# Half of the late wide cross's keys made earlier, in the narrow cross, and kept in DRAM until they are used

## The reference, cut to what matters

```python
# layer 0, second block: narrow cross attention, 16 heads of 8
q = layernorm(x) @ Wq0.T + bq0;  k = ctx @ Wk0.T + bk0;  v = ctx @ Wv0.T + bv0
x = x + softmax(q k / sqrt(8) + mask) v @ Wo0.T + bo0
...                       # feed-forward of layer 0, two narrow self attentions
# layer 1: wide cross attention, 16 heads of 64, inner width 1024
q = layernorm(x) @ Wq + bq;  k = ctx @ Wk + bk;  v = ctx @ Wv + bv
x = x + softmax(q k / 8) v @ Wo + bo
x = x + tanh(layernorm(x) @ W + bias)      # last block, in the same stage
```

## Time and profile before

| what | value |
|---|---|
| runs | 2460.63, 2465.46, 2465.57 us, median 2465.46 |
| the profiled execution: its time | 2466.49 us |
| its span, first to last instruction | 2464.7 us |
| mean granted TensorE clock | 0.949 of full speed |
| wide cross | about 1708 to 2465 us of the span |
| narrow cross | about 548 to 911 us of the span |

### The profile page before, as it was taken

One profiled execution on the slowest core, in us unless ns is written; L12 is line 12 of the kernel. 1 busy time (PEld: TensorE's weight loads), 2 busy tenths in 40 slices (PEclk: granted clock), 3 DMA queues, 4 the chain that ended last, 5 costly groups with the idle time before them and its releaser, 6 DMA issues. The chain is left out here.

```text
span 2464.7 us, 90437 instructions
## 1 busy us (share of the span) xinstructions
PE 2193.9 (89%) x33039; PEld 1802.1 (73%) x33039; DVE 1921.8 (78%) x5481; ACT 1509.8 (61%) x3973; POOL 1225.4 (50%) x1215
## 2 busy tenths in 40 slices
PE   8999999988777753439999799998999999999998
PEld 7888888875555541228888678886888888888886
DVE  3888888868999986988888667775777778777785
ACT  0666666657777766538888678885344444444443
POOL 0333333327777763019999699995223223232232
PEclk8999999998999996659999899999999999999999
DMA  4000000001111100010000000000000000000000
GB/s 122 3 0 0 0 0 0 0 4 34 30 31 30 29 17 1 1 34 2 0 0 0 1 2 0 0 0 4 9 12 12 13 11 13 11 11 13 11 12 15
DMA packets 66160, 29.87 MB, mean 12 GB/s; under 512 B 19139, under 2 KB 65542, under 8 KB 66054
## 3 DMA queue, kind: packets, MB, share of 16 engines
q1 hardware_dynamic: 62642, 27.26, 4.1%
q10 hardware_dynamic: 3412, 1.19, 0.2%
HBM read 20.04 MB, written 8.39 MB: 12 GB/s over the span
## 5 line engine op out<-in xcount | busy, mean ns | idle before, releaser
L706 POOL TENSOR_TENSOR sa_sc<-sa_sc,sa_rs 128x1024 f32<-128x1024 f32 x64 | 121.9, 1904 | 317.3 <-DVE sa_rs L682 317.3
L1861 POOL TENSOR_TENSOR lo_qk_r<-lo_qk_ms,w_neg_half 128x20 f32<-128x20 f32 x64 | 226.7, 3543 | 22.0 <-DVE lo_qk_ms L1784 21.9
L1861 POOL TENSOR_TENSOR gl_qk_r<-gl_qk_ms,w_neg_half 128x20 f32<-128x20 f32 x64 | 226.9, 3545 | 1.4 <-DVE gl_qk_ms L1784 1.4
L486 POOL TENSOR_TENSOR xan_ve<-xan_mv,w_eps_ln 128x1 f32<-128x1 f32 x64 | 12.1, 189 | 400.2 <-DVE xan_mv L480 400.2
L889 ACT ACTIVATE xan_xT<-xa_misc 128x128 f32<-128x128 f32 x64 | 17.7, 277 | 297.9 <-PE xa_misc L789 267.3
L1012 POOL TENSOR_TENSOR xa_sc<-xa_sc,xa_rs 128x1024 f32<-128x1024 f32 x64 | 121.7, 1901 | 112.2 <-DVE xa_rs L972 112.2
L818 PEld LDWEIGHTS xa_qs<-xan_xT,late_x_wq 128*128 128x128 f32 x1024 | 120.0, 193 | 53.3 <-issue 53.3
L558 PE MATMUL sa_qs<-san_xT,w_a_wq 128*128 128x128 f32 x1024 | 132.2, 284 | 2.6 <-DVE sa_sc L668 2.2
L818 PE MATMUL xa_qs<-xan_xT,late_x_wq 128*128 128x128 f32 x1024 | 132.1, 282 | 0.6 <-DVE xa_sc L963 0.6
L829 PE MATMUL xa_pp<-xa_cT,late_x_wk 128*128 128x128 f32 x1024 | 131.1, 281 | 0.0
L926 ACT ACTIVATE xa_oT<-xa_oo 128x512 f32<-128x512 f32 x128 | 69.4, 594 | 97.6 <-PE xa_oo L865 97.6
(11 more groups left out here) (329 smaller groups left out, 6878.1 us busy)
## 6 DMA issues: line engine op xcount, KB each, us to landing
w_x<-in_x_dram SPq DMA_DIRECT2D x8, 512.0 KB, 7.6
ca_cx<-in_ctx_dram SPq DMA_DIRECT2D x64, 64.0 KB, 1.8
ctxT_kept<-ca_xcT SPq DMA_DIRECT2D x64, 64.0 KB, 1.6
xa_cT<-ctxT_kept SPq DMA_DIRECT2D x64, 64.0 KB, 1.8
out_dram<-xa_out SPq DMA_DIRECT2D x64, 64.0 KB, 1.6
ca_mask<-in_mask_BxSxS_ff_dram SPq DMA_DIRECT2D x64, 32.0 KB, 1.7
w_a_wq<-in_L_attn_Wq_dram SPq DMA_DIRECT2D x1, 512.0 KB
w_a_wo<-in_L_attn_Wout_dram SPq DMA_DIRECT2D x1, 512.0 KB
```

The lines of the kernel that those rows point to most:

```text
L706: pool.tensor_tensor(v, v, bcast(rs[:, s, :], 2, S), ALU.mult).then_inc(prob_done, 1)
L1861: pool.tensor_tensor(qk_r[:, s, :], qk_ms[:, s, :], k["neg_half"][:, 0:NQK], ALU.pow).then_inc(sg["qk_r"], 1)
```

## The change

PE's `keys` in the wide cross makes only the lower four of the eight 128-column blocks; the upper four (columns 512 to 1023) are made in the narrow cross by a new piece `ahead`, copied from PSUM by ACT (`ahead_keys`), stored by SP (`keep_keys`) to a new DRAM buffer of 256 KB per tile, and loaded back by SP in the wide cross (`load_keys`). There DVE adds their bias from SBUF instead of PSUM.

```diff
 wide cross, SP
                 def load(t, s):
-                    after(sp, k_psum, t, 2, per=2)
-                    after(sp, v_psum, t, 2, per=2)
+                    after(sp, k_psum, t, 2)
...
+                def load_keys(t, s):
+                    after(sp, k_done, t, 2, per=2)
+                    sp.dma_start(ak[:, s, :], k["aheadK"][at, :]).then_inc(ak_in[s], 16)
...
-                skewed(sp, NT, [(0, load), (10, store)])
+                skewed(sp, NT, [(0, load), (0, load_keys), (10, store)])
 wide cross, PE
-                    for b in range(2):
-                        after(pe, p_done, t, 2, per=2)
-                        for c in range(4):
-                            ch = 4 * b + c
-                            final = pe.matmul(pp[b][:, c * P:(c + 1) * P], k["x_wk"][:, ch * P:(ch + 1) * P],
-                                             cT[:, s, :], start=True, stop=True)
-                        final.then_inc(k_psum, 1)
+                    after(pe, p_done, t, 2, per=2)
+                    for c in range(4):
+                        final = pe.matmul(pp[0][:, c * P:(c + 1) * P], k["x_wk"][:, c * P:(c + 1) * P],
+                                         cT[:, s, :], start=True, stop=True)
+                    final.then_inc(k_psum, 1)
 wide cross, DVE
                     after(dve, s_psum, t, 2)
-                    for b in range(2):
-                        dve.wait_ge(k_psum, t * 2 + b + 1)
-                        dve.tensor_tensor(kT[:, s, 4 * b:4 * b + 4, :], pp[b][:, :].rearrange("p (c i) -> p c i", c=4),
-                                          bcast(k["x_bk"][:, 4 * b:4 * b + 4], 2, P), ALU.add).then_inc(k_done, 1)
+                    landed(dve, ak_in, t, s)
+                    dve.tensor_tensor(kT[:, s, 4:8, :], ak[:, s, :].rearrange("p (c i) -> p c i", c=4),
+                                      bcast(k["x_bk"][:, 4:8], 2, P), ALU.add).then_inc(k_done, 1)
+                    after(dve, k_psum, t)
+                    dve.tensor_tensor(kT[:, s, 0:4, :], pp[0][:, :].rearrange("p (c i) -> p c i", c=4),
+                                      bcast(k["x_bk"][:, 0:4], 2, P), ALU.add).then_inc(k_done, 1)
 narrow cross, SP
+                def keep_keys(t, s):
+                    after(sp, ak_done, t)
+                    sp.dma_start(k["aheadK"][at, :], ak[:, s, :]).then_inc(ak_out[s], 16)
+                sp.dma_start(wk[:, :], k["dram"]["L1_xattn_Wk"][:, 512:1024]).then_inc(wk_in, 16)
-                skewed(sp, NT, [(2, keep), (0, load)])
+                skewed(sp, NT, [(2, keep), (0, load), (3, keep_keys)])
...
 narrow cross, PE
+                def ahead(t, four):
+                    s = four % 2
+                    after(pe, xT_done, t)
+                    after(pe, ak_done, t, 1)
+                    after(pe, p_done, t, 4, per=2)
+                    for n in range(4):
+                        last = pe.matmul(pp[0][:, n * P:(n + 1) * P], wk[:, n * P:(n + 1) * P], xcT[:, s, P:2 * P], start=True, stop=True)
+                    last.then_inc(ak_psum, 1)
...
                 def turn_probs(t, four):
                     after(pe, exp_done, t)
+                    pe.wait_ge(ak_done, min(t + 4, NT) if isinstance(t, int) else t + 4)
...
-                skewed(pe, NT, [(3, scores), (2, project), (1, turn), (6, attend), (5, turn_probs), (7, output)], 4)
+                pe.wait_ge(wk_in, 16)
+                skewed(pe, NT, [(3, scores), (2, project), (2, ahead), (1, turn), (6, attend), (5, turn_probs), (7, output)], 4)
 narrow cross, ACT
                     after(act, qkv_psum, t, 2)
+                    after(act, ak_psum, t, 2)
                     landed(act, kept, t, s, 2)
...
+                def ahead_keys(t, four):
+                    s = four % 2
+                    after(act, ak_psum, t)
+                    landed(act, ak_out, t, s, 2)
+                    act.activation(ak[:, s, :], pp[0][:, :], ACT.Copy).then_inc(ak_done, 1)
...
-                skewed(act, NT, [(2, queries_keys), (1, turned), (2, values), (4, exponent), (5, probsT), (0, apply)], 4)
+                skewed(act, NT, [(2, queries_keys), (2, ahead_keys), (1, turned), (2, values), (4, exponent), (5, probsT), (0, apply)], 4)
 build
+    k["aheadK"] = nc.dram_tensor("ahead_keys", (tiles * P, 512), F32, kind="Internal").ap()
```

More of the change, by code:

```diff
@@ L726, in wide_cross_attention @@
         cT = sb("cT", [P, 2, P])
+        ak = sb("ahead_keys", [P, 2, 512])
         qT = sb("qT", [P, 2, 8, P])
@@ L742, in wide_cross_attention @@
         ctx_in = [sem(f"ctx_in{s}") for s in range(2)]
+        ak_in = [sem(f"ahead_in{s}") for s in range(2)]
         q_psum, q_done, k_psum, k_done, v_psum, v_done = sem("q_psum"), sem("q"), sem("k_psum"), sem("k"), sem("v_psum"), sem("v")
@@ L752, in load @@
                 def load(t, s):
-                    after(sp, k_psum, t, 2, per=2)
-                    after(sp, v_psum, t, 2, per=2)
+                    after(sp, k_psum, t, 2)
                     at = slice(t * P, (t + 1) * P) if isinstance(t, int) else bass.ds(t * P, P)
                     sp.dma_start(cT[:, s, :], k["ctxT"][at, :]).then_inc(ctx_in[s], 16)
+                def load_keys(t, s):
+                    after(sp, k_done, t, 2, per=2)
+                    at = slice(t * P, (t + 1) * P) if isinstance(t, int) else bass.ds(t * P, P)
+                    sp.dma_start(ak[:, s, :], k["aheadK"][at, :]).then_inc(ak_in[s], 16)
                 def store(t, s):
@@ L1045, in narrow_cross_attention @@
         off = sb("off", [P, 2])
+        wk = sb("x_wk_half", [P, 512])
+        ak = sb("ahead_keys", [P, 2, 512])
         m1, m2 = ps("m1"), ps("m2")
@@ L1052, in narrow_cross_attention @@
         kept = [sem(f"kept{s}") for s in range(2)]
+        wk_in, ak_psum, ak_done = sem("x_wk_in"), sem("ahead_psum"), sem("ahead_keys")
+        ak_out = [sem(f"ahead_out{s}") for s in range(2)]
         zeroed, one = sem("zeroed"), sem("ones")
@@ L1074, in keep @@
                     sp.dma_start(k["ctxT"][at, :], xcT[:, s, P:2 * P]).then_inc(kept[s], 16)
-                skewed(sp, NT, [(2, keep), (0, load)])
+                def keep_keys(t, s):
+                    at = slice(t * P, (t + 1) * P) if isinstance(t, int) else bass.ds(t * P, P)
+                    after(sp, ak_done, t)
+                    sp.dma_start(k["aheadK"][at, :], ak[:, s, :]).then_inc(ak_out[s], 16)
+                sp.dma_start(wk[:, :], k["dram"]["L1_xattn_Wk"][:, 512:1024]).then_inc(wk_in, 16)
+                skewed(sp, NT, [(2, keep), (0, load), (3, keep_keys)])
                 for s in range(2):
                     sp.wait_ge(kept[s], 16 * len(range(s, NT, 2)))
+                    sp.wait_ge(ak_out[s], 16 * len(range(s, NT, 2)))
             @block.tensor
```

## The result

The changed kernel takes 2576.10 us (median of 2572.67, 2576.10, 2579.24), against 2465.46 before: 1.0456 times as long, 95% interval 1.044 to 1.0471, 110.6 us slower. The forecast was 2607 us with a range of 2548 to 2670. The profiled execution took 2579.24 us, its span is 2577.5 us.

The account below looks back on a forecast made before the run. PE was taken to fill the wide cross, with DVE's chain close behind; 2466.5 + 145 (store's ring, narrow cross) - 3 (wide cross) - 1 (median below profiled execution) = 2607 us, 5.8% slower, range 2548 to 2670.

Parts of the forecast that it names:

- What bounds the kernel now: Wide cross: PE's stream fills the 11.46 us step, with DVE's chain 0 to 0.15 us behind.
- The store's ring: Narrow cross: ACT's copy waits for a store queued behind the mask's wait; step 7.68 us against 5.30, 145 us in all.
- landing of a 256 KB store: Narrow cross, term of the store's ring: taken as 2.4 us, between a 64 KB store's 1.6 and a 512 KB load's 3.6.
- rival D: Narrow cross: PE's clock falls to half as PE gets less busy; 104 us more if throughout, 2711 us; chance 10%.
- The other ring of the narrow cross: Narrow cross: ahead waits for the probsT copies and delays turn; 0.6 us a step, 5.9 instead of 5.3.
- rival B: Narrow cross: the store's ring doesn't bind, only the ring over probsT and ahead costs 38 us; 2500 us; chance 9%.
- The wide cross: Wide cross: removing four key matmuls, 0.95 us a step, gains only DVE's slack; 3 us taken, 0 to 16 possible.
- the "nothing" for it: Wide cross: DVE's key half read from SBUF instead of PSUM gains 0 to 2 us; nothing taken.
- PE would stand 0.9 us ahead of the scores: Wide cross, sign in the changed profile: PE idle about 0.9 us ahead of scores, released by DVE's kT; steps of 11.4 us.
- A: Wide cross: all 61 us of removed key matmuls come back, while the store's ring holds; 2549 us; chance 6%.
- C: Faster kernel: wide cross gives back 61 us and the narrow cross loses less; 2443 us; chance 4%.
- the granted clock in the narrow cross isn't 1.00: Narrow cross: sign named beforehand that would show the forecast wrong, PE's clock not staying full.

Follow-up runs that it names:

- e6: The kernel before, with DVE doing keys ahead of apply and apply_last in the wide cross: 2458.62 us, 0.9988 times before.
- e2: The wide cross of the change with the narrow cross of before; upper key blocks not made, weights loaded in their place: 2456.90 us, 0.9974 times before.
- e1: The changed kernel with SP's store of the keys put ahead of the mask DMA in the narrow cross: 2471.87 us, 1.0030 times before.
- e8: The changed narrow cross with the wide cross of before, four slots for made keys instead of two, SP's order left: 2477.35 us, 1.0054 times before.
- e10: e9 with PE's turn_back ahead of output in the wide cross: 2438.54 us, 0.9896 times before.
- e9: The changed kernel with the edits of e1 and e5 together: 2450.86 us, 0.9947 times before.
- e4: The changed kernel with DVE's keys ahead of its two normalisings in the wide cross: 2550.57 us, 1.0351 times before.
- e5: e4 with the halves of DVE's keys exchanged, the one from PSUM first, then the one from SBUF: 2547.59 us, 1.0355 times before.

## Why the prediction was right, and where its sizes were off

*What bounds the kernel now.* Right. e6 fits PE's stream setting the step of the wide cross before, and e2 shows that DVE's chain is within 6.8 / 63 = 0.11 us of it (0.13 in the changed kernel); the slack that I gave was 0 to 0.15 us.

*The store's ring.* The mechanism was right in each link, shown by e1 and e8, which each open it at one place. Its terms against the changed kernel's timeline: `turn_probs` and `output` 1.32 and 1.29; release 0.15 and 0.15; `residual` to softmax 0.86 and 0.95; softmax 1.29 and 1.29; release of the mask DMA 0.20 and 0.17; to the store 0.56 and 0.56; copy 0.60 and 0.60; release of PE 0.15 and 0.09. The term that was mis-sized is "landing of a 256 KB store ... I take 2.4", with the 0.15 for ACT's release: 2.55 us, measured 2.13, from the store's start to ACT's (median landing 2.1). The straight line was drawn from a small store to a large load, and loads land later than stores here: 256 KB take 2.8 us as a load of the wide cross and 2.1 us as a store. The step was 7.68 by the sum and is 7.22 where it is regular; over 61 steps that is 28 us too much.

*How near the total came is in part luck.* The stage grew by 124.6 us, 20 less than the 145 forecast, not 28 less. Two things that the sum didn't have lie between. The 11 steps from 573.62 to 666.11 took 8.41 us instead of 7.22, 13 us more (rival D below). And the ring began later than counted: the first four steps took 4.93 us each, where the sum has two at 5.30 and then 7.68. Of the 31 us by which the forecast lay too high, 20 are this stage, 5 the wide cross (8.2 for the 3 taken), 3.6 the rest of the program, and 2 are that the profiled execution lies 3 us above its median and not 1.

The Trainium skill's page "DMA: Bandwidth & Descriptors", section "Anatomy of one DMA — SWDGE (gpsimd) path", would have given 2.6 us for 256 KB on GpSimd's path, an estimate by its figures. The store from SP's queue lands in 2.1 us here (64 KB in 1.6), so for this queue the measurement decides.

*The other ring of the narrow cross*, "0.6 us a step, 5.9 instead of 5.3": the mechanism is there but it adds 0.27 us by the means (5.57 for 5.30, e1 and e8); it was hidden in the result and moved no number of the forecast except rival B's, whose 2500 us would have been about 2475.

*The wide cross.* "I take 3 us": 8.2 by the trace, 6.8 by e2. The loop's release was taken as 0.26 us from another stage's; here it was 0.10, as in the steps written with constants, which leaves 0.15 us of slack a step. The SBUF half cost 0.67 us, as much as the PSUM half, so the "nothing" for it was right in the place that it had. The forecast that PE would stand 0.9 us ahead of the scores was wrong. By the starts of one step (2190.50 to 2201.82, against the earlier trace rows), the keys take 0.90 us less (0.99 where PE doesn't wait behind them, as in e10, for 1.89), and 0.37 us come back ahead of the scores, 0.29 ahead of `output` and 0.10 in `output` itself. The step that failed is that of asking only what the removed matmuls did for PE, and not what they covered: ACT's `outT` (e10).

*The rivals.* A and C, the 61 us in full: ruled out by e2. B: ruled out by ACT's wait. D: it came true in part, in the first steps of the ring, and the sign "the granted clock in the narrow cross isn't 1.00" stood there. Windows of the changed kernel, then two of its steps, each from ACT's copy on:

```profile
565.00:660.00 95.00, 63.88 (x940) 50.47 (x939) 49.85 (x96) 52.48 (x136) 46.71 (x56) 0.87 0.18 56
660.00:1010.00 350.00, 250.33 (x4352) 197.37 (x4352) 225.21 (x436) 226.72 (x583) 194.97 (x241) 1.00 0.18 58
```

```profile
592.10 0.60 ACT L1211 ACTIVATE ca_ahead_keys<-ca_pp 128x512 f32<-128x512 f32 x1 [4.50 <-DMA ahead_keys<-ca_ahead_keys]
...
592.80 1.82 PE L1165 MATMUL ca_pp<-w_constant,ca_sc 128*128 128x128 f32 x8 [3.72 <-issue]
...
600.26 0.60 ACT L1211 ACTIVATE ca_ahead_keys<-ca_pp 128x512 f32<-128x512 f32 x1 [2.48 <-DMA ahead_keys<-ca_ahead_keys]
...
600.96 1.06 PE L1165 MATMUL ca_pp<-w_constant,ca_sc 128*128 128x128 f32 x8 [1.71 <-issue]
```

From 575 us on the kernel before had 1.00. Here PE stood 3.72 us, then ran at the lower level, 1.2 GHz (the windows of 593 to 596 us have 0.50), and `turn_probs` took 1.82 us instead of 1.06; in the next step it had stood 1.71 us and ran at 2.4 GHz. The long stand was the store's: it had started at 587.91, 4.19 us ahead of ACT's copy, against 2.13 in the regular steps. In the 11 long steps these late landings make up 10 of the 13 us (the sum of what each lies over 2.12), and about 3 are left for the lower clock. Why stores land late in just these steps no run shows.

*What stays open.* The late landings at the start of the ring, and the 0.21 us in `output` of e10, as said. And whether `ahead` in PSUM of its own, clear of `pp0`, would bring the narrow cross back to 5.30 us a step. All eight banks are in use, and its blocks would have to share one that PE writes for other work while ACT reads; that wasn't tried.

## What to carry to other kernels

When a transfer is added to a queue, ask which waits stand ahead of it in that queue, which event of which step they need, and in which step its slot is wanted again: here a store sat behind a wait that had cost nothing, and two slots weren't enough to hide it. When work is taken off a full engine, look for the second chain behind it and for what the work had covered; here a freer DVE alone gave at most 5 us (e6), the removed matmuls alone 7 (e2), and the two together, with the orders of e9 and e10, 27 (e10). An idle time that the profile books as "issue" is to be read beside the end of the operation whose semaphore is waited for.

## What the runs showed of the hardware

An operation of DVE with its inputs in SBUF is held while POOL's tensor operation runs: 1.46 us instead of 0.68 when it starts 0.91 us ahead of POOL's end (e4), 0.78 when it starts 0.23 ahead (e5), both ending 0.55 us behind POOL; and 0.99 instead of 0.33 for the normalising in its old place, which ends 0.08 us behind POOL's operation; while an operation with one input in PSUM takes its 0.69 us beside the same POOL operation. The Trainium skill's page "SBUF — State Buffer", section "Who interferes with whom", says that DVE and GpSimd share a pair of ports that whoever starts first holds for its whole instruction, that a DVE operation on two tensors takes part only with both inputs in SBUF and against a GpSimd operation that reads SBUF, and that one on a tensor and scalars can do so in certain fast modes. The durations agree with it; whether the normalising ran in such a mode no row shows. The held time shows as busy time of the DVE instruction, not as idle time. So 0.66 us of the 0.99 was this wait, and in e4 it passed to the SBUF half of the keys, which came first there.

The same 256 KB from or to DRAM on SP's queue landed in 2.1 us as a store and 2.8 us as a load (medians), and a store in up to 4.1 us, in the first steps of the changed narrow cross (2.0/2.1/4.1 as its shortest, median and longest).
